# Output weight's parts and the first block's values and reciprocals, put into the tile of attention's first k stack during attention's last unit

## The reference, cut to what matters

```python
q, k, v = ...                    # 16 heads of 32, rotary on q and k
a = softmax(einsum('bhik,bhjk->bhij', q, k))
y = einsum('bhij,bhjv->bhiv', a, v).transpose(0, 2, 1, 3).reshape(b, l, d)
x = x + y @ wo
h2 = layer_norm(x, mlp_ln_scale)
h2 = gelu(h2 @ w1) @ w2          # 512 -> 2048 -> 512
return x + h2
```

## Time and profile before

| what | value |
|---|---|
| median of 3 runs | 3582.47 us (3579.41 to 3586.3) |
| the profiled execution | 3573.79 us |
| its span, first to last instruction | 3572.0 us |
| mean granted TensorE clock | 0.979 |
| PE busy | 3420.8 us (96%) |
| DVE, POOL, ACT busy | 58%, 56%, 42% |
| DMA share from 2000 to 2150 us | 0.50 |

### The profile page before, as it was taken

The page is one execution under the profiler, slowest core; times in us unless marked ns, Lnnn a source line. Parts: engine busy times, 40 slices in busy tenths (PEclk is TensorE's granted clock), DMA queues, the critical chain, the costliest instruction groups (busy, mean ns, idle before and its releaser), DMA issues. The chain is left out here.

```text
span 3572.0 us, 47047 instructions
## 1 busy us (share of the span) xinstructions
PE 3420.8 (96%) x16632; PEld 2230.6 (62%) x16632; DVE 2079.4 (58%) x3331; ACT 1508.5 (42%) x2785; POOL 2016.5 (56%) x1613
## 2 busy tenths in 40 slices
PE   6999899999999999999999959999999995999998
PEld 5777455454554555545455348888888883778877
DVE  6776677777777777777777344222222213454554
ACT  2332466666666666666666632111111112222221
POOL 3644488887978888797888812222222223343342
PEclk9999999999999999999999979999999997999999
DMA  5556677869678686867865543122222114222221
GB/s 193 177 169 205 118 154 138 148 129 154 140 131 152 127 156 133 151 142 132 156 127 107 113 140 107 55 73 75 73 67 75 54 36 139 83 86 76 73 87 41
DMA packets 176737, 419.32 MB, mean 117 GB/s; under 512 B 15382, under 2 KB 62998, under 8 KB 151670
## 3 DMA queue, kind: packets, MB, share of 16 engines
q1 hardware_dynamic: 153606, 249.59, 26.4%
q0 software_dynamic: 22896, 166.73, 24.0%
HBM read 162.25 MB, written 87.03 MB: 70 GB/s over the span
## 5 line engine op out<-in xcount | busy, mean ns | idle before, releaser
L868 DVE TENSOR_REDUCE part_max<-ps_att 128x1 f32<-128x512 f32 x1972 | 1225.4, 683 | 372.2 <-PE ps_att L786 372.1
L914 ACT ACTIVATE probs<-ps_att 128x512 f32<-128x512 f32 x2048 | 1061.7, 603 | 521.9 <-PE ps_att L758 458.7
L965 POOL TENSOR_TENSOR prob_sums<-prob_sums,probs 128x512 f32<-128x512 f32 x884 | 1142.8, 1537 | 60.8 <-DMA probs<-probs 60.8
L810 PE MATMUL ps_att<-probs,v_tok 128*32 128x512 f32 x4096 | 548.3, 607 | 3.1 <-DMA v_tok<-v 3.1
L1456 POOL TENSOR_TENSOR ff_g_lo<-ff_g,ff_g_hi 128x512 fp32r<-128x512 f32 x128 | 164.7, 1287 | 551.5 <-DVE ff_g_hi L1417 551.5
L758 PE MATMUL ps_att<-q_stack,k_stack 97*128 97x512 f32 x768 | 319.8, 424 | 9.9 <-ACT probs L914 9.7
L758 PE MATMUL ps_att<-q_stack,k_first 97*128 97x512 f32 x768 | 324.7, 423 | 2.6 <-ACT probs L914 2.6
L1325 ACT ACTIVATE ff_g<-ps_ff 128x512 f32<-128x512 f32 x128 | 76.5, 597 | 582.2 <-PE ps_ff L1209 582.2
L786 PE MATMUL ps_att<-k_stack,q_stack 96*128 96x512 f32 x768 | 303.8, 396 | 0.0
L786 PE MATMUL ps_att<-k_first,q_stack 96*128 96x512 f32 x756 | 301.9, 399 | 0.0
L1946 POOL TENSOR_TENSOR av_gated_lo<-av_full,av_gated_hi 128x512 fp32r<-128x512 f32 x64 | 94.4, 1475 | 313.9 <-ACT av_gated_hi L1783 313.9
(11 more groups left out here) (209 smaller groups left out, 5514.9 us busy)
## 6 DMA issues: line engine op xcount, KB each, us to landing
probs<-probs POOLq DMA_DIRECT2D x159, 1024.0 KB, 8.6
q_stack<-qk SPq DMA_DIRECT2D x144, 128.0 KB, 6.9
qk<-rot_hi SPq DMA_DIRECT2D x64, 256.0 KB, 7.0
qk<-rot_lo SPq DMA_DIRECT2D x64, 256.0 KB, 5.0
av_gate_rows<-gate SPq DMA_DIRECT2D x64, 256.0 KB
k_stack<-qk SPq DMA_DIRECT2D x24, 512.0 KB, 10.4
k_first<-qk SPq DMA_DIRECT2D x18, 512.0 KB, 10.1
x_in_sb<-in_x SPq DMA_DIRECT2D x8, 1024.0 KB, 6.7
```

The costliest lines, as they stand in the source:

```text
L810: mm = nc.tensor.matmul(o_ps[rows, :], t["v"][:, steps[w]["b"], k, rows], t["p"][:, w % PR, h, :], start=(k == 0), stop=(k == LT - 1))
L868: nc.vector.tensor_reduce(t["pm"][:, r, k:k + 1], mx[mx_uses % 3], AX.X, ALU.max)\
L914: nc.scalar.activation(t["p"][:, at % PR, h, :], sT[(at * G + h) % 3], ACT.Exp)\
L965: nc.gpsimd.tensor_tensor(x, first, t["p"][:, w % PR, h, :], ALU.add).then_inc(s["acc_done"], 1)
```

## The change

The tile of `k_first` gets 128 partitions and, with `q_first`, lives until the end of `feed_forward`. Its four heads' slices serve in the last unit of attention, which does not read them as K. `prepare` copies the output weight in DRAM to `wo_copy`, 1 MB, behind the third load of x. In the last unit the queue loads `wo_copy` into slice 2 at step 2, ACT casts it into slice 0 in four pieces behind the exponentials of steps 8 to 11, and DVE takes the rest into slice 1 after the last maxima. The sums are loaded at step 40 in place of 46 and the reciprocals stored at step 49 in place of 55. Then the values of the first block (1 MB) go into slice 2 and its reciprocals (four loads of 256 KB) into slice 3. `feed_forward` uses slices 0 and 1 as output weight and 2 and 3 as `ff_h_hi` and `ff_h_lo`, and `q_first` for the GELU's parts. Its own loads of output weight, first values and first reciprocals and its four splits are gone, and x stands third in its queue. The splits of the first eight MLP pieces are laid out anew: four at steps 12 to 15 of turn -1 (they were at 4 to 7), four at step 0 of block 0 (they were at 8 to 11), and all later pairs one step later.

```diff
+                sp.dma_start(a["wo_copy"], a["wo"]).then_inc(s["wo_kept"], 16)
...
+    wo_hi, wo_lo, y_raw, y_rl = (t["k0"][:, i, :] for i in range(4))
+    wo_raw = y_raw
...
-                if at == end - 18:
+                if unit == UNITS - 1 and w == 2:
+                    sp.dma_start(wo_raw.bitcast(F32), a["wo_copy"].rearrange("p k n -> p (k n)")).then_inc(s["wo_in"], 16)
+                if unit == UNITS - 1 and w == 40:
                     sp.wait_ge(s["l_stored"], 16 * (blocks - 3))
...
-                if at == end - 9:
+                if unit == UNITS - 1 and w == 49:
                     sp.wait_ge(s["recip"], 1)
...
+                if unit == UNITS - 1 and w == 52:
+                    sp.wait_ge(s["wo_lo"], DC)
+                    sp.wait_ge(s["y_stored"], 16 * ((UNITS - 2) * NB + 1))
+                    sp.dma_start(y_raw.bitcast(F32).rearrange("p (k t) -> p k t", k=DC),
+                                 a["yT"].rearrange("(k p) t -> p k t", p=P)[:, :, 0:TB]).then_inc(s["first_in"], 16)
+                if unit == UNITS - 1 and w == 54:
+                    sp.wait_ge(s["rl_stored"], 16)
+                    for f in range(DC):
+                        src = a["rl"][f * G:(f + 1) * G, 0:TB].unsqueeze(1).broadcast_to([G, KD, TB])
+                        sp.dma_start(y_rl[:, f * TB:(f + 1) * TB].bitcast(F32), src).then_inc(s["first_in"], 16)
...
+            sp.wait_ge(s["first_in"], 16 * (DC + 1))
...
-                if at == end - 12:
+                if at >= end - 17 and at < end - 17 + DC:
+                    i = at - (end - 17)
+                    dve.wait_ge(s["wo_hi"], i + 1)
+                    cols = slice(i * D, (i + 1) * D)
+                    nc.vector.tensor_tensor(wo_lo[:, cols], wo_raw[:, cols].bitcast(F32), wo_hi[:, cols].bitcast(F32),
+                                            ALU.subtract).then_inc(s["wo_lo"], 1)
+                if at == end - 18:
                     dve.wait_ge(s["l_in"], 16)
...
+                if st["unit"] == UNITS - 1 and 8 <= st["w"] < 8 + DC:
+                    i = st["w"] - 8
+                    act.wait_ge(s["wo_in"], 16)
+                    cols = slice(i * D, (i + 1) * D)
+                    nc.scalar.activation(wo_hi[:, cols], wo_raw[:, cols].bitcast(F32), ACT.Copy).then_inc(s["wo_hi"], 1)
...
-        woh, wol = sb("wo_hi", [P, DC, D], F32R), sb("wo_lo", [P, DC, D], F32R)
+        woh, wol, hh, hl = (t["k0"][:, i, :].rearrange("p (k n) -> p k n", k=DC) for i in range(4))
+        x = t["x"]
+        gh, gl = t["q0"][:, 0:2], t["q0"][:, 2:4]
...
-                return [m] if 4 <= m < WOUT + 2 * WQ else []
-            first = WOUT + 2 * WQ + 2 * m
+                return [WOUT + m - (MC - WQ)] if m >= MC - WQ else []
+            if n == 0 and m == 0:
+                return list(range(WOUT + WQ, WOUT + 2 * WQ))
+            first = WOUT + 2 * WQ + 2 * (m - 1)
...
-                for i in range(4):
-                    load_chunk(i)
-                load_first(0)
                 load_x(0)
-                load_first(1)
-                for i in range(4, 8):
+                for i in range(WOUT, WOUT + 4):
                     load_chunk(i)
...
-                for i in range(WOUT):
-                    chunk_hi(i)
...
-                                pool.wait_ge(s[f"y_first{j // 2}"], 16 * (DC + 1))
```

More of the change, by code:

```diff
@@ L1406, in _ @@
                 nc.vector.tensor_tensor(awl[:], awr[:], awh[:].bitcast(F32), ALU.subtract).then_inc(s["aw_lo"], 1)
-                for i in range(WOUT):
-                    chunk_lo(i)
                 for n in turns:
@@ L1984, in program @@
             attention(nc, c, a, t)
-        if stop >= 2:
-            feed_forward(nc, c, a)
-        if stop >= 4:
-            average(nc, c, a)
+            inner.close()
+            t["x"] = kept("rows", [P, TT, D])
+            feed_forward(nc, c, a, t)
+        average(nc, c, a)
 def rows(w):
```

47 lines of the change are left out of this document (19 added, 28 removed).

## The result

The changed kernel takes 3549.34 us (median of six runs, 3542.67 to 3562.17). The kernel before takes 3580.55 us beside it (six runs, 3577.69 to 3586.30). The ratio is 0.9915, with a 95% interval of 0.9896 to 0.9935. That is 31.2 us less, where 17.9 were forecast.

The account below looks back on a forecast made before the run. PE was taken as the bound, full within feed-forward blocks but idle where attention ends; 22.3 us gained less 2.1, 2.0 and 0.3 gave 17.9 us off the 3582.5 us median: 3565 us forecast, range 3556 to 3575.

Parts of the forecast that it names:

- 22.3 - 2.1 - 2.0 - 0.3 = 17.9 us: Sum: fourth projection 22.3 us earlier, less 2.1 and 2.0 given back at two places, 0.3 for ACT's casts in attention.
- Start of the first projection: Feed-forward start: with the loads and splits gone, PE starts at 2067.7 in place of 2082.76, 15.0 us gained.
- First to second projection: Distance between the first two projections' starts: 5.7 us in place of 11.43, another 5.7 us gained.
- Second to fourth: Second to fourth projection: two periods of 3.96 us, 7.9 in place of 9.6, 1.6 us gained.
- Given back, first place: Behind the normalization: three weight splits ahead of DVE's lower parts delay the third transpose and first MLP matmul, 2.1 us lost.
- Given back, second place: First step of the block: four weight splits behind the first GELU make PE stand before the first down matmuls, 2.0 us.
- Rival A: Feed-forward start: the load of x is the next wait, landing at 2077.2; costs 4.6 us, gain 13.3, 3569 us; chance 0.13.
- Rival B: MLP's first steps: moved splits make the next weight pieces load late, ACT stands before third GELU; gain 10 to 14; chance 0.12.
- Rival C: Attention's last unit: new loads slow POOL's paired additions, 8.6 us late with 4.9 free; 3.7 us lost, 3568 us; chance 0.08.
- Rival D: Slower: the weight's copy in DRAM at the start holds up the rotated rows' stores, costing its excess over 12.6 us; chance 0.04.

Follow-up runs that it names:

- the kernel with the early splits: Changed kernel with the first eight MLP weight splits moved: four to the third and fourth projections' steps, four behind the first block's low parts; 3544.34 us, ratio 0.9886.

## Why the prediction was wrong

The direction was right, and so was the mechanism of the gain that it counts: up to the first down matmul 17.9 us were forecast and 15.9 measured. The time lies outside the range because one step is missing.

- **The step that failed** is the one that closes the sum: "22.3 - 2.1 - 2.0 - 0.3 = 17.9 us", with "the rest unchanged" after the second up matmul. The move of `ff_h_hi`, `ff_h_lo` and the GELU's parts into the old stacks was costed at nothing: "`feed_forward` uses slices 0 and 1 as output weight and 2 and 3 as `ff_h_hi` and `ff_h_lo`" was read as a matter of space. But it also changed where the two operands of each MLP matmul lie to each other, from 32 to 0 modulo 256 bytes, and with it the pitch from 233 to 227 ns. That is worth 16 to 18 us: 18.1 on the MLP phase where it was done alone, by the order of the tiles, and 16.4 where one tile of 32 bytes undid it. The prediction named no such term, and none of its rivals would have brought a time below its range.
- **Start of the first projection**: 15.0 us forecast, 12.1 measured. The 3.0 are the phase's later beginning (first issue 2067.63 against 2064.60). The term took attention's end as fixed. It said of DVE's subtractions that "nobody in attention waits for them". But the queue waits for them, and behind it the store of the sums, and behind that ACT. In the kernels where DVE was done some 16 us earlier, 2.5 of these came back.
- **First to second projection**: 5.7 us apart forecast, 5.73 measured. **Second to fourth**: 1.6 us forecast. It took 7.69 in place of 9.56, so 1.9.
- **Given back, first place**: 2.1 us forecast, 1.95 measured (19.66 at the fourth projection, 17.71 at the first MLP matmul), behind the named part on DVE.
- **Given back, second place**: 2.0 us forecast, a wait of 2.24 measured, with `w_lo` as its releaser. But it costs about 4 in all, since the granted clock is at 1.2 GHz for 3.4 us behind it. The forecast counted only the pause.
- **Rival A** did not come: x landed 5.7 us after its issue, and DVE's first addition waited for PE, not for `rows`. (The 6.7 us that the prediction took are of the first stage's loads, not of the phase before.) **Rival B**: ACT did wait 2.28 us for `ff_z` at 2108.20, but PE was busy with slow matmuls and did not stand for it. **Rival C**: its mechanism came at half its size, and cost nothing. The paired addition issued at 2041.78, with the new loads, landed after 12.0 us, and its counterpart before after 7.9. POOL waited 6.18 us for it (until 2053.82) and ended at 2058.81, ahead of its reader at 2059.60: 4.1 us late, of which 4.9 were free. Attention's last unit, from its first exponential to its last matmul, took 203.9 us before and 203.7 in the changed kernel, with ACT's four casts in it, though attention as a whole varied by up to 17 us between kernels. **Rival D**: the first stage's last matmul ends at 382.03, and before at 381.72, so the copy in DRAM cost at most 0.3. It took 14.7 us to land where 8.6 were assumed, but it was issued at 31.61, 16 us ahead of the first store.

In all: 12.1 at the start and 7.6 more up to the fourth projection are 19.7, less 2.0 and 1.8 at the two places gives 15.9 at the first down matmul. From there to the end of the phase another 15.7. In the kernel with the early splits, which has the same pitch and no wait there, the same stretch is 17.5 us shorter than before, so the 15.7 are the pitch's 17.5 less 1.8 for the clock. The rest after the phase is unchanged within 0.5.

## What to carry to other kernels

When a change moves tiles, compare the distance between the starts of groups of matmuls in stretches where nothing was touched. A busy share of 100% hides a difference of 2%, and the count of instructions in a fixed window shows it. Where PE bounds a stage, lay out stationary and moving operand with starts that are equal modulo 256 bytes, by pads or the order of tiles, and measure it. A wait that a queue is given for an engine's result is paid by everything behind it, so count that as well, and a pause of PE with the clock behind it: here 2.24 us cost about 4.

## What the runs showed that was not expected

- With fp32r operands of 128x128 and 128x512, PE's matmuls start every 227 ns when the two start at the same place modulo 256 bytes, and every 231 to 235 (medians) when they differ by 32, 64 or 128 (3197 to 3216 against 3263 to 3269 in 700 us). Other differences were not tried in the MLP. The last stage showed it too (2108 to 2136 in 500 us), and so did the distances in the projections and the first stage, though the first stage got no shorter. Attention, with operands of 97 rows, did not get shorter by its pad. What in the chip causes it was not tried. The Trainium skill, TensorE: Matmul & The Clock Gate, section "Back-to-back issue gap", gives an isolated gap by the columns alone, some 216 ns for 512 at full clock, some 131 ns for 512 in a sustained stream, and nothing on where operands lie. The runs show 227 at best.
- DVE's subtraction and its float32 copy, from and to SBUF, stood up to 16.6 us beside an unbroken row of additions on POOL. The reciprocal did not.
- The issue of the four loads of the reciprocals took the queue 9.93 to 10.56 us in every kernel that has them behind the load of the values, and 2.31 to 2.50 us in the three that have them ahead of it. Why was not tried.
- The attention stage, with the same instructions, took from 1672 to 1689 us in the profiled executions, and its last unit from 203.7 to 204.1 in all of them. A difference of a few us is better read from the distances within a profile than from the time.
